# A new slot table for the five engines of a four-stage transformer kernel, with a few edits to its setup

## The reference

```
x = LN(x + attention(x))       # 16 heads of 16 features that share one key and one value head
x = LN(x + ffn(x))             # 256 -> 1024, exact gelu, 1024 -> 256, weights ternary
x = LN(x + ssm_cfc(x))         # inner LN, decay scan over positions, then a recurrence over 512 steps:
                               #   h = ff1*(1-t) + t*ff2, ff1/ff2 tanh, t sigmoid, each of [x_t, h]
x = LN(x + quantised_linear(x))  # both operands rounded to an fp6 grid in blocks of 32
```

## Time and profile before

| | |
|---|---|
| median of 3 runs | 1886.12 us (1884.8 to 1889.21) |
| profiled execution | 1886.12 us, span 1884.4 us from first to last instruction |
| mean granted TensorE clock | 0.974 of full speed |
| busy share of the span | PE 93%, PE weight load 68%, DVE 76%, ACT 62%, POOL 55% |
| chain that ended last | PE 66%, DVE 12%, POOL 10%, issue 5%, DMA 3% |

### The profile page before, as it was taken

How to read it: one execution, slowest core, us unless ns; L and a number is a source line. 1 busy time by engine, 2 the same in 40 slices (tenths; PEclk the granted TensorE clock), 3 DMA queues, 4 the chain that set the end, 5 groups by cost and what they waited for, 6 DMA issues and landing times.

```text
span 1884.4 us, 74521 instructions
## 1 busy us (share of the span) xinstructions
PE 1758.8 (93%) x29935; PEld 1279.9 (68%) x29935; DVE 1437.1 (76%) x2995; ACT 1166.6 (62%) x2795; POOL 1035.3 (55%) x3194
## 2 busy tenths in 40 slices
PE   6689999999999999999999999999999999999975
PEld 4445567777777777777777777767777777777653
DVE  4657767788777877787778877887788778877554
ACT  3356656666666666666666666666666666666621
POOL 4202255666565666566566656666656665665632
PEclk8889999999999999999999999999999999999975
DMA  9511111111111111111111111111111111111000
GB/s 244 133 39 38 38 45 39 39 49 47 45 41 45 50 43 43 42 51 44 45 39 49 46 46 39 46 48 44 41 45 50 43 46 39 50 45 27 23 25 21
DMA packets 140912, 92.94 MB, mean 49 GB/s; under 512 B 20196, under 2 KB 139800, under 8 KB 140568
## 3 DMA queue, kind: packets, MB, share of 16 engines
q1 hardware_dynamic: 136368, 87.91, 17.5%
q10 hardware_dynamic: 4200, 0.27, 0.2%
HBM read 31.50 MB, written 18.35 MB: 26 GB/s over the span
## 4 chain that ended last, share of the span: by engine, by line
PE 66%; DVE 12%; POOL 10%; issue 5%; DMA 3%; SPq 2%; ACT 1%; DVEq 0%; POOLq 0%; ACTq 0%
PE gen_bank L767 12%; PE value_bank L730 9%; PE gen_bank L869 8%; PE score_bank L698 8%; PE max_banks L560 6%; DVE nmax L1122 4%; PE gate_bank L762 4%; PE gen_bank L582 3%; PE gen_bank L808 2%; PE gen_bank L836 2%; PE gen_bank L777 2%; PE gate_bank L746 2%; POOL x2s L1608 2%; POOL diff L1666 2%; DVE stats L1243 2%
## 5 line engine op out<-in xcount | busy, mean ns | idle before, releaser
L1069 ACT ACTIVATE probs<-score_bank 128x512 f32<-128x512 f32 x1024 | 589.9, 597 | 289.0 <-PE score_bank L698 279.6
L1122 DVE TENSOR_REDUCE nmax<-max_banks 128x2 f32<-128x1024 f32 x512 | 620.1, 1211 | 63.8 <-PE max_banks L562 61.8
L698 PE MATMUL score_bank<-qaug,kaug 98*128 98x512 bf16 x1024 | 370.0, 384 | 1.2 <-DMA qaug<-nmT 0.9
L730 PE MATMUL value_bank<-probs,vaug 128*32 128x128 f32 x8192 | 330.7, 279 | 0.0
L1666 POOL TENSOR_TENSOR diff<-gates 128x16 f32<-128x16 f32 x472 | 126.9, 269 | 331.9 <-ACT gates L1075 331.0
L730 PEld LDWEIGHTS value_bank<-probs,vaug 128*32 128x32 f32 x8192 | 192.9, 109 | 127.4 <-issue 103.2
L767 PE MATMUL gen_bank<-w2T,hT 128*128 128x256 f32 x1024 | 265.4, 392 | 0.0
L560 PE MATMUL max_banks<-kaug,qaug 64*128 64x512 bf16 x512 | 198.6, 388 | 41.0 <-DVE nmax L1122 36.0
L767 PEld LDWEIGHTS gen_bank<-w2T,hT 128*128 128x128 f32 x1024 | 184.0, 189 | 52.1 <-issue 27.6
L1075 ACT ACTIVATE gates<-gate_bank 128x48 f32<-128x48 f32 x472 | 99.2, 210 | 188.6 <-PE gate_bank L762 181.1
L562 PE MATMUL max_banks<-kaug,qlow 64*128 64x512 bf16 x512 | 199.6, 390 | 0.0
(11 more groups left out here) (233 smaller groups left out, 2998.1 us busy)
## 6 DMA issues: line engine op xcount, KB each, us to landing
qstage<-qpiece SPq DMA_DIRECT2D x384, 64.0 KB
lowstage<-qpiece SPq DMA_DIRECT2D x192, 64.0 KB
xt<-in_L_attn_x SPq DMA_DIRECT2D x64, 128.0 KB
xk<-in_L_attn_x SPq DMA_DIRECT2D x16, 512.0 KB, 7.5
residual<-x2s SPq DMA_DIRECT2D x64, 128.0 KB
x2f<-residual SPq DMA_DIRECT2D x64, 128.0 KB
out<-x SPq DMA_DIRECT2D x64, 128.0 KB
raw<-in_L_ffn_W SPq DMA_DIRECT2D x2, 1024.0 KB, 12.3
```

Source lines behind the costliest of these rows:

```text
L698: pe.matmul(score_bank[t % 2][:, :], kaug[0:AUG, r, tt, u, :], qaug[:, r, u, :, :].rearrange("p h s -> p (h s)"), start=True, stop=True).t ...
L730: last = pe.matmul(value_bank[32 * g:32 * g + 32, :].rearrange("p (k t) -> p k t", k=HG)[:, :, uv * BLOCK_POS:(uv + 1) * BLOCK_POS], vaug[ ...
L1069: act.activation(probs[:, t % 4, :], score_bank[t % 2][:, :], ACT.Exp).then_inc(exp_done, 1)
L1122: dve.tensor_reduce(nmax[:, m % 2, at:at + 3:2], max_banks[:, :, :], AX_X, ALU.max, negate=True).then_inc(max_taken, 1)
```

## The change

Most entries of the four tables get other slots, so the engines do the same work in another order. Outside the tables: in the setup DVE runs its setup parts and the ordering of queries ahead of the maximum of the same b, and the bias adds come at b = 13 instead of 14; the operand of the gate biases is kept on 9 partitions instead of 128 rows with zeros, which drops one memset and one wait. No instruction of a tile time is added or removed.

```diff
@@ -32,10 +32,10 @@
 )
 
 
-PE_AT = dict(XT=29, INPUT=5, Q=0, OUT=23, OT=13, ATT=22, PROJ=28, TURNX=32, B=41, X1T=48, NM=46, FFN1A=56, FFN1B=61, TURND=74, LAST=79, F2_0=62, F2_1=63, F2_2=63, F2_3=64, F2_4=64, F2_5=71, F2_6=71, F2_7=71)
-ACT_AT = dict(XT=31, OT=7, Q=5, ATT=22, Q8=60, TURNX=35, X1T=49, TURND=71, GELUA=56, GELUB=58)
-DVE_AT = dict(Q=0, X2R=13, X3R=25, X2=13, OT=13, X3=58, QUANT=61, XN=25, ORDER=36, LN1=25, X1=47, BS=45, SCAN=59, X1P=50, NM=55, X4R=87, X4=112)
-POOL_AT = dict(LN2=11, LN3=38, PIECES=8, X2S=37, QIN=59, XD=63, X3B=56, LN1=34, X1B=55, LN4=92, LNI=21)
+PE_AT = dict(XT=23, INPUT=4, Q=0, OUT=27, OT=12, ATT=20, PROJ=23, TURNX=32, B=45, X1T=48, NM=49, FFN1A=56, FFN1B=62, TURND=76, LAST=79, F2_0=64, F2_1=64, F2_2=64, F2_3=64, F2_4=67, F2_5=70, F2_6=71, F2_7=71)
+ACT_AT = dict(XT=23, OT=1, Q=0, ATT=17, Q8=62, TURNX=30, X1T=49, TURND=71, GELUA=57, GELUB=59)
+DVE_AT = dict(Q=1, X2R=10, X3R=29, X2=18, OT=14, X3=62, QUANT=62, XN=25, ORDER=37, LN1=27, X1=43, BS=45, SCAN=60, X1P=49, NM=52, X4R=86, X4=105)
+POOL_AT = dict(LN2=11, LN3=50, PIECES=0, X2S=19, QIN=54, XD=63, X3B=60, LN1=39, X1B=63, LN4=89, LNI=18)
 TAIL = dict(OUT=0, X3R=0, LN3=0, STATS3=1, X3=3, X3B=4, QMAX=4, QSCALE=5, QIN=6, Q8=7, XD=8, TURN=9, COPY=9, LAST0=10, LAST1=11, X4R=11, STATS4=12, LN4=12, X4=14, INPUT=1)
 TAIL_SSM = dict(F2=0, X2R=0, LN2=0, X2=2, X2S=2, XN=4, TURN=4, COPY=4, B=5, BS=5, SCAN=6)
 
@@ -158,9 +158,9 @@
         bias_piece = sb("bias_piece", [P, 3, 3])
         bias_rest = sb("bias_rest", [P, 2, 3])
         bias_bf = sb("bias_bf", [P, 2, 3], BF16)
-        bias_rows = sb("bias_rows", [P, P], BF16)
-        gate_ones = sb("gate_ones", [P, STEPS, 3, B])
-        gate_of = sb("gate_of", [P, STEPS, 3, B], BF16)
+        bias_rows = sb("bias_rows", [9, P], BF16)
+        gate_ones = sb("gate_ones", [9, STEPS, 3, B])
+        gate_of = sb("gate_of", [9, STEPS, 3, B], BF16)
         apow = sb("apow", [P, S])
         ainv = sb("ainv", [P, S])
         small = sb("small", [P, 32])
@@ -684,7 +684,7 @@
                 max_pair(0, pair)
             pe.wait_ge(v_kept, R)
             pe.wait_ge(bias_rows_made, 1)
-            pe.wait_ge(gate_made, 5)
+            pe.wait_ge(gate_made, 4)
 
             def tile_time(c, r, n):
                 for t in range(TICKS):
@@ -1009,8 +1009,7 @@
                     act.activation(gcT[:, :, :], gate_bank[:, 0:3 * P].rearrange("p (g n) -> p g n", g=3), ACT.Copy).then_inc(product_out, 1)
                 if b == 17:
                     act.wait_ge(bias_turned, 1)
-                    act.wait_ge(gate_made, 5)
-                    act.activation(bias_rows[0:9, :], gate_bank[0:9, 0:P], ACT.Copy).then_inc(bias_rows_made, 1)
+                    act.activation(bias_rows[:, :], gate_bank[0:9, 0:P], ACT.Copy).then_inc(bias_rows_made, 1)
 
             def tile_time(c, r, n):
                 g0, g1 = gen_bank
@@ -1183,7 +1182,7 @@
                     link(dve.tensor_tensor(wfb, fq[:, :].rearrange("p (j i) -> p j i", i=QBLOCK),
                                            fs[:, 2, :].unsqueeze(2).to_broadcast([P, nblk, QBLOCK]), ALU.mult))
                     assert made[0] == F_QUANTISED
-                if b == 14:
+                if b == 13:
 
                     dve.wait_ge(bias_sums, 1)
                     dve.wait_ge(setup_pool, 3)
@@ -1229,11 +1228,11 @@
                     split_keys(b // GROUP - 1)
                 if b == SECOND + 1:
                     rest_piece(1)
-                if b in range(FIRST_MAX, FIRST_MAX + TICKS // 2):
-                    take_maxima(0, b - FIRST_MAX)
                 setup_part(b)
                 if b in (7, 15):
                     order_queries((b - 7) // 8)
+                if b in range(FIRST_MAX, FIRST_MAX + TICKS // 2):
+                    take_maxima(0, b - FIRST_MAX)
             for pair in range(B + MORE - FIRST_MAX, TICKS // 2):
                 take_maxima(0, pair)
             dve.wait_ge(decay_step, DECAY_STEPS + 1)
@@ -1490,9 +1489,8 @@
                                pattern=[[0, STEPS], [3, 3], [0, B]], channel_multiplier=-1).then_inc(gate_made, 1)
             pool.wait_ge(gate_made, 3)
             pool.tensor_copy(gate_of[:, :, :, :], gate_ones[:, :, :, :]).then_inc(gate_made, 1)
-            pool.memset(bias_rows[:, :], 0.0).then_inc(gate_made, 1)
-
-            pool.wait_ge(gate_made, 5)
+
+            pool.wait_ge(gate_made, 4)
 
             def more_pieces(m):
```

## The result

The changed kernel takes 1904.88 us (median of 4 runs, 1899.13 to 1907.02), the kernel before 1885.46 us in the same session; the ratio is 1.0095, 95% interval 1.0067 to 1.0121. It is slower by about 19 us, where the forecast was 13 us faster, and it lies above the top of the range. The profiled execution took 1905.95 us, span 1904.2 us.

What follows compares the result with a forecast made beforehand. PE bounds a steady tile time (busy 25.95 of 26.55 us), with DVE's maxima a step behind. Terms -9.7 - 1.5 - 1.4 - 2.4 + 2.5 = -12.5 from 1886.12 give 1873.6, stated as 1873 us; range 1852 to 1900.

Steps and rivals of the forecast that it cites:

- Nine partitions: Gate-bias product on PE, one per tile time: costs nothing; 6 us if a whole 0.1 us weight load showed.
- The first score product: Tile time's first score product, waiting for two small transfers: they land at 3.6 to 4.0 us, cost nothing.
- rival A: Small transfers land late, first score product waits 0.5 us in 54 tile times: +27, 1900 us; chance 0.18.
- DVE's chain: Ticks 5 to 13: DVE's maxima bind, 10.68 us to FFN1A; 26.50 us a tile time, 9.7 us less over 54.
- relief: DVE's ordering copy shortens once POOL's X2S no longer lies over it: 0 to 0.41 us, taken as 0.2.
- places without slack: Allowance in the steady tile time: 0.1 us added to 26.4, giving 26.50.
- a sign against it: Forecast is wrong if DVE picks up a new wait in ticks 5 to 13; no size given.
- End of the tile time: FFN1B, GELUB, exp 15 up to tick 1's score product: PE arrives at 7.4 us, cost nothing, no slack left.
- Rival D: Exp 15 on ACT more than 0.5 us late: 1915 us and more; chance 0.03.
- about as much at a recurrence step: PE's idle time in the tile time's second half: about 0.26 us at a recurrence step.
- Setup and first tile times: Before the steady part: setup 1.5 us less, n = 0 and 1 1.4 less, n = 2 to 5 2.4 less.
- Tail: After the last tiles: eight F2 instead of five and uncovered exp 15 cost 2.5 us more; bounds -1 and +5.

Runs made afterwards that it cites:

- e1: The changed kernel with the bias operand back on 128 partitions (added rows zero); 1886.64 us, 0.9987 of the kernel before.
- e2: The kernel before with the bias operand on 9 partitions and nothing else; 1907.11 us, 1.0097 of the kernel before.
- e11: The changed kernel with the bias operand on 65 partitions and F2_0 to F2_2 at slot 63; 1873.38 us, 0.9928 of the kernel before.
- e12: The changed kernel, operand still on 9 partitions, with F2_0 to F2_2 at slot 63; 1891.55 us, 1.0018 of the kernel before.
- e5: The changed kernel with operand on 128 partitions and F2_0 to F2_2 back from slot 64 to 63; 1871.64 us, 0.9916 of the kernel before.

## Why the prediction was wrong

**The step that failed** is "Nine partitions": "a weight load there lies behind other work ... Nothing; should it cost a whole weight load of 0.1 us, 6 us." Measured: 18.2 us between e1 and the changed kernel, 0.97% in e2, and 18.2 us between e11 and e12, two kernels of one session that differ in the operand alone. In the profiles of e1 and the changed kernel it is 19.2 us by parts: 0.29 us in most tile times (26.82 against 26.53), which is 15.7 over 54 but 13.4 in their sum, as fewer of them waited for the small transfers; 1.0 ahead of the first INPUT; and 4.8 in the rest (215.8 against 211.0). The duration of the load was right and was the wrong question: what changed is what may lie under what. The row that could have priced it was there before, 0.23 us ahead of every load on the whole array behind a 64-row pair; the prediction read PE's products at those places and not its weight loads. Its upper bound of 6 us was taken from a duration and not from a wait.

**The first score product.** "I take the landing at 3.6 to 4.0, near the idle value, cost nothing; bounds 0 and 1.3 us a tile time." The price was inside the bounds: 12.3 us in e1 (54 times 26.746 - 26.519). It came otherwise than rival A had it. The large transfers do leave earlier, and in most tile times the landing is on time: in e5 the second lands 3.6 us after FFN1A in the median, as forecast; about every third to fourth is late by up to 1.2 us. Read as a mean the term is 0.23 us, just under the 0.25 from which rival A would decide. The prediction's "no steady landing was under 2.3" holds for its rows of 800 to 1000 us; over the whole steady part of the kernel before the shortest is 1.7.

**DVE's chain.** Forecast 10.68 us without relief, 0.2 of relief, 0.1 for places without slack. Measured from the pair of tick 5 (965.79) to FFN1A (976.44) 10.65: 0.43 + 3.72 + 2.28 + 2.28 + 1.94. The relief came whole (2.28 in place of 2.70), and 0.17 and 0.18 us of it went into the two last steps, the first of them mostly X1's wait for POOL's rstd (0.15), a new wait of DVE of the kind that the prediction had named as a sign against it. With 128 rows the tile time is 26.53 where 26.50 was forecast, and with the score product covered the 54 take 8.6 us less than before; forecast 9.7. The waits were where they were said to be: pairs of ticks 9 and 11 wait 0.3 us for the maxima, the turn of xn not at all.

**End of the tile time.** Costed at nothing with no slack left, and that held: the tick 1 product starts at 983.82, 7.38 us after FFN1A (forecast 7.4), right behind exp 15. Rival D's price does not follow from its condition: exp 15 half a microsecond late would cost 54 x 0.5 = 27 us and give 1900 us, not 1915; nothing hangs on it. The recurrence steps' wait for POOL, 21.5 us over the steady part before, is gone (0.3); the prediction had it only as "about as much at a recurrence step".

**Setup and first tile times.** POOL's long pass starts at 57.16 (forecast 56.5), the first score product of n = 0 at 91.82 (forecast 91.5). Together -6.6 us at the first INPUT, forecast -5.3; the runs with the new tables give -6.6 to -11.5, so this fit is no closer than that scatter.

**Tail.** Forecast +2.5, bounds -1 and +5. The tables cost +4.5 (211.0 against 206.5); 2.0 of it is the three extra F2 (211.0 against 209.0 in e5), the remainder was not taken apart. The changed kernel has another 4.8 (215.8 against 211.0): 1.1 in the four tile times up to n = 64 and 3.7 behind them. There the granted clock differs too. The windows from the INPUT of n = 64 to the end, the changed kernel and e1:

```profile
1792.16:1904.24 112.08, 73.41 (x1366) 52.08 (x1366) 57.11 (x242) 21.11 (x78) 40.81 (x108) 0.65 0.07 21
```

```profile
1776.69:1885.03 108.34, 68.79 (x1366) 49.37 (x1366) 57.04 (x242) 21.18 (x78) 40.90 (x108) 0.70 0.08 21
```

The clock is 0.65 of full speed in the mean against 0.70, so PE has more time at the lower of its two levels, 1.2 GHz. What of the 3.7 us is the clock and what the five INPUTs there, no run separates.

So the forecast of 1873 us describes a kernel with the operand on 65 rows or more and F2 ahead of the score product (1871.6 us); the two terms left at nothing, 18 and 12 us (in the changed kernel itself 8.3 of waits, 13.3 against e12), and the tail's 2 us above its estimate make up the difference. That the kernel before and e1 take nearly the same time is no sign that the tables do nothing: it is a gain of 16 us (e5, 0.84%) of which the new wait takes 13. The range failed because its top came from rival A alone: no case had the operand itself costing more than 6 us.

## What to carry to other kernels

When an edit changes the height or width of a TensorE operand, look for the idle time ahead of the weight loads at existing places where the same change of size occurs, and price a change there and back by it, less the idle time that stands at the new place already (here 0.23 + 0.17 - 0.01 - 0.12 = 0.27 us, against 0.29 measured); fewer rows saved nothing here and cost 1%. Where products of another size are needed, put them next to each other or at a place where the size changes anyway. Work that stands ahead of a product that waits for a small transfer is cover for its worst landing: price its removal with the late landings, not the median one.

## What the runs showed of the hardware

- The price has a step: 65 and 96 rows run like 128, 64 and 9 rows cost the same 0.29 us for the change there and back (most tile times 26.53 or 26.54 against 26.82 or 26.83). A second 9-row product behind the first costs 0.17 us, as on 128 rows (0.16).
- The weight load's own length hardly depends on the rows: 91 ns with 9, 93 with 64, 95 with 65, 97 with 128. The profile books the change as idle time for "issue", in PE's load rows and in no product's row.
- The second of two 4 KB transfers landed 1.7 to 2.1 us after its issue, and 2.2 to 3.8 in the tile times in which a 16 KB packet of the instruction queue started beside them (e5; counted, not moved).
- A DVE copy of 96x2048 bf16 took 1.10 us with a POOL operation on 128x256 f32 over it (43 of 43, the X2S of the kernel before) and 0.69 without it (20 of 21).
